# Layer 1's experts on the rows that chose them, for six of eight batches of a two-layer adaLN transformer

## What is computed

```python
h = layernorm(x) * (1 + ca) + sa
x = x + ga * attn1(h)              # 16 heads of 8 channels, relative bias, gate
h = layernorm(x) * (1 + cb) + sb
x = x + gb * ffn1(h)
# ffn1: a causal latent attention (MLA), then a mixture of 8 experts
def ffn1(x):
    x = x + mla(rmsnorm(x, g1))
    x = x + moe(rmsnorm(x, g2))
def moe(t):                        # t: tokens x 128
    top_v, top_i = top_k(t @ gate_w, 2)
    gates = softmax(top_v)
    combine = zeros(T, 8).at[rows, top_i].add(gates)
    hid = silu(einsum('td,edh->teh', t, w1))   # w1: 8 x 128 x 256
    ye = einsum('teh,ehd->ted', hid, w2)       # w2: 8 x 256 x 128
    return einsum('te,ted->td', combine, ye)
```

## Time and profile before

| what | us |
|---|---|
| median of 3 timed runs | 1957.47 |
| lowest and highest timed run | 1955.97 and 1969.35 |
| the profiled execution | 1974.12 |
| its span, first to last instruction | 1972.3 |
| first score matmul of slot 0, from the span's start | 692.2 |

### The profile page before, as it was taken

One profiled execution on the slowest core, in us unless ns is written; L12 is line 12 of the kernel. 1 busy time (PEld: TensorE's weight loads), 2 busy tenths in 40 slices (PEclk: granted clock), 3 DMA queues, 4 the chain that ended last, 5 costly groups with the idle time before them and its releaser, 6 DMA issues.

```text
span 1972.3 us, 46460 instructions
## 1 busy us (share of the span) xinstructions
PE 1737.1 (88%) x17489; PEld 1159.2 (59%) x17489; DVE 1428.1 (72%) x4507; ACT 1000.2 (51%) x2018; POOL 625.6 (32%) x871
## 2 busy tenths in 40 slices
PE   3898889898939479989999999999999999998997
PEld 2676767777726346545655655655555555655455
DVE  6777877787721267877887886887887787788756
ACT  2554455455513146647546636646645645644642
POOL 3111221111134147625514613613623522530000
PEclk6999999999969779979999999999999999999999
DMA  4522122211018222122212213123122122221111
...
DMA packets 109933, 144.31 MB, mean 73 GB/s; under 512 B 18752, under 2 KB 90880, under 8 KB 108432
## 3 DMA queue, kind: packets, MB, share of 16 engines
...
## 4 chain that ended last, share of the span: by engine, by line
PE 51%; DVE 11%; issue 3%; ACT 2%; DMA 1%; SPq 1%; ACTq 1%; POOL 1%; DVEq 0%; POOLq 0%
PE ps L1969 10%; PE ps L1954 8%; PE ps L2110 6%; PE ps L2008 5%; PE ps L2124 5%; PE ps L2019 4%; PE ps L1979 3%; DVE ps L2198 2%; PE ps L1225 2%; PE ps L1234 1%; DVE l_XY L2198 1%; PE ps L1981 1%; PE ps L2059 1%; DVE l_xn L2236 1%; PE ps L2039 1%
## 5 line engine op out<-in xcount | busy, mean ns | idle before, releaser
L1773 POOL TENSOR_SCALAR l_XY<-l_XY,l_nmax 128x512 f32<-128x512 f32 x512 | 388.8, 768 | 224.3 <-DVE l_nmax L2198 215.8
L2198 DVE CUSTOM_DVE_ANT_0 l_XY<-ps,strips 128x512 f32<-128x512 f32 x512 | 341.1, 687 | 140.6 <-PE ps L1954 136.8
L1954 PE MATMUL ps<-l_stack 72*128 72x512 bf16 (+3 forms) x1024 | 353.9, 351 | 65.7 <-DVE l_nmax L2198 53.8
L1830 ACT ACTIVATE PT<-ps 128x512 f32<-128x512 f32 x512 | 305.1, 599 | 197.4 <-PE ps L1969 184.7
L1969 PE MATMUL ps<-ident,l_XY 128*128 128x128 f32 x2048 | 319.0, 278 | 3.8 <-POOL l_XY L1773 3.0
L1969 PEld LDWEIGHTS ps<-ident,l_XY 128*128 128x128 f32 x2048 | 240.3, 141 | 110.5 <-ACT PT L1830 45.5
L2198 DVE CUSTOM_DVE_ANT_0 ps<-ps,mask 128x384 f32<-128x384 f32 (+3 forms) x512 | 245.2, 504 | 31.0 <-PE ps L1954 27.0
L1954 PEld LDWEIGHTS ps<-l_stack 72*128 72x128 bf16 x1024 | 102.0, 100 | 148.6 <-DVE l_nmax L2198 84.3
L1979 PE MATMUL ps<-l_stack 75*128 75x256 bf16 (+3 forms) x512 | 157.7, 310 | 13.1 <-ACT PT_odd L1838 6.0
L1838 ACT ACTIVATE PT_even<-ps 128x512 f32<-128x512 f32 (+1 forms) x256 | 120.9, 493 | 67.2 <-PE ps L1981 56.7
L2110 PE MATMUL ps<-l_fT,l_w_e 128*128 128x512 f32 x256 | 146.0, 659 | 2.6 <-DVE l_hid L2386 1.2
...
## 6 DMA issues: line engine op xcount, KB each, us to landing
...
l_w_e<-in_L_ffn_w_dram ACTq DMA_DIRECT2D x128, 128.0 KB
...
```

What stands on the lines that cost most here:

```text
L1773: nc.gpsimd.tensor_scalar(XY[:, c % XY_BUFS], XY[:, c % XY_BUFS], -1.0, nmax[:, c % 8:c % 8 + 1], ALU.mult, ALU.add).then_inc(y_pool, 1)
L1830: nc.scalar.activation(PT[:, quad(u, r), j], src.rearrange("p (k q) -> p k q", q=P), ACT.Exp).then_inc(moved, 1)
L1954: nc.tensor.matmul(ps[:, n % 3, 0:w], stack[0:STACK, 0, h, q * P:(q + 1) * P], stack[0:STACK, 1, h, 0:w], start=True, stop=True).then_inc( ...
L2198: nc.vector.tensor_tensor_reduce(out=dst, in0=src, in1=add, scale=-1.0, scalar=3.0e38, op0=ALU.add, op1=ALU.min, accum_out=low).then_inc(s ...
```

## The change

Batches 0 to 5 no longer run the experts densely. The rest of layer 1's mathematics is the same, and batches 6 and 7 keep the dense form.

1. **Router alone.** For a batch below 6 the place in the schedule holds only the projection, normalisation, logits and top-2 (`router`). A `fold` adds the scaled residual to `x` at once. New small VectorE operations and two or three bf16 matmuls count how many rows each expert has so far (`tally`, `place`), which gives each row two places in a DRAM tensor `rows_dram`. Eight indirect DMAs per batch on GpSimd scatter the 512 normalised rows there twice. Batch 2 and batch 5 have their router earlier, at place 38 of slots 7 and 13.
2. **Plan.** After the last router of a group (batches 0 to 2, then 3 to 5), five steps of VectorE work (`plan_blocks`) turn the counts into a list of 32 blocks: which 128 rows and which expert. 24 full blocks would hold 3072 rows; eight more cover the part-filled last block of each expert.
3. **Block pairs.** 16 pairs of blocks per group run in kind-1 slots, one pair every four steps: eight in slot 8, eight in slot 10, and 16 from place 18 of slot 14 to place 21 of slot 15. SP reads two numbers per block from the plan into registers and issues one DMA for 128 rows (64 KB) and one for the expert's weights (256 KB) from a table that it has copied together in DRAM. A pair is two transposes, eight fp32 matmuls of 128 columns (two records each), two ScalarE copies of 128x256, one tanh of 128x512, one VectorE product of 128x512, and a 128 KB store issued by ScalarE.
4. **Gather and add.** For each of the six batches, eight indirect DMAs on GpSimd bring the two results per row back, and VectorE weights and adds them: batches 0, 1, 2 in slot 12, batches 3 and 4 in slot 15, batch 5 after the last tile.
5. **Clearing and table.** SP clears `rows_dram` in six DMAs of 2 MB and builds the weight table (2 MB), in slots 0 to 5.
6. **Values.** `PT` has two buffers instead of three; the third one's memory holds part of the new tiles. `values` takes one buffer per call: the same number of column passes in matmuls of 128 columns instead of 256, twice as many instructions, one burst of 32 records every four steps instead of two bursts of 16 in every eight.
7. **SP's order.** SP's program follows the steps too, with the pair loads between `stack_up` and `store_parts`.

```diff
-MOE_START = {b: TILES * PLACE[1, b + 1] - 6 for b in range(B - 2)}
+GROUPS = ((0, 1, 2), (3, 4, 5))
+DENSE = (B - 2, B - 1)
+EARLY = [batches[-1] for batches in GROUPS] + list(DENSE)
+MOE_START = {b: TILES * PLACE[1, b] + TURN_AT[1] + 1 if b in EARLY else TILES * PLACE[1, b + 1] - 6 for b in range(B)}
...
+PAIR_STAGES = dict(load=-9, turn=0, evac=1, hidden=3, tanh=4, mul=5, out=6, copy=7)
+PAIR_WINDOWS = ((0, TILES * PLACE[1, 3] + 18, 8, 4), (0, TILES * PLACE[1, 4] + 18, 8, 4), (1, TILES * PLACE[1, B - 2] + 18, 16, 4))
...
+CLEAR_AT = (40, TILES + 20, 2 * TILES + 40, 3 * TILES + 50, 5 * TILES + 50)
+TABLE_AT = TILES + 40
+COMBINE = {0: TILES * PLACE[1, 5] + 2, 1: TILES * PLACE[1, 5] + 18, 2: TILES * PLACE[1, 5] + 34,
+           3: TILES * PLACE[1, B - 1] + 31, 4: TILES * PLACE[1, B - 1] + 47, 5: ALL + 2}
...
-V_AT, W_AT = 13, 32
+V_AT, W_AT = 10, 32
-XY_BUFS, QUADS, W_BUFS, VW = 5, 3, 3, HD + 2
+XY_BUFS, QUADS, E_BUFS, VW = 5, 2, 3, HD + 2
...
 # SP
+                def load_block_pair(n):
...
+                    wait_turned(sp, ("T", before))
...
+                    if n >= W_BUFS:
+                        sp.wait_ge(block_y_ready, n - W_BUFS + 1)
+                    for k in range(2):
+                        j = 2 * i + k
+                        at = nc.values_load(plan[0:1, g % 2, 0, j:j + 1], engines=(mybir.EngineType.SP,), ...
+                        e = nc.values_load(plan[0:1, g % 2, 1, j:j + 1], engines=(mybir.EngineType.SP,), ...
+                        sp.dma_start(x_b[:, n % X_BUFS, k, :], rows_dram[bass.ds(at, 1)]...
+                        sp.dma_start(w_b[n % W_BUFS][:, k, :], table_dram[bass.ds(e, 1)]...
...
 # GpSimd
+                def scatter(b, part):
...
+                    nc.gpsimd.indirect_dma_start(rows_dram.rearrange("n p c -> (n p) c"),
+                                                 bass.IndirectOffsetOnAxis(ap=row_index[:, k, t:t + 1], axis=0),
+                                                 xf[:, t, :], None, bounds_check=REGION_ROWS - 1,
...
 # TensorE
+                def block_hidden(n, m):
+                    pe.wait_ge(block_x_moved, n + 1)
...
+                    for i in range(2):
+                        for f in range(FT1):
+                            last = nc.tensor.matmul(ps[:, SIDE, (2 * i + f) * P:(2 * i + f + 1) * P],
+                                                    w_b[n % W_BUFS][:, i, f * P:(f + 1) * P], xT_b[:, n % 2, i, :], start=True, stop=True)
...
-                    for k in (2 * r, 2 * r + 1):
+                    for k in range(TT):
                         for j in range(4):
-                            last = nc.tensor.matmul(o[32 * j:32 * j + VW], v[:, k, 4 * head_group(s, g) + j, :], pair[:, :, j, k, :],
+                            last = nc.tensor.matmul(o[32 * j:32 * j + VW], v[:, k, 4 * head_group(s, g) + j, :], PT[:, quad(u), j, k, :],
...
 # ScalarE
-                for n in range(W_BUFS):
-                    expert(n)
...
+                def block_exponent(n):
+                    act.wait_ge(block_hid_ready, n + 1)
...
+                    nc.scalar.activation(hid_b[:, n % 2].rearrange("p i f s -> p (i f s)"), ps[:, SIDE, :], ACT.Tanh,
+                                         scale=0.5).then_inc(block_tanh, 1)
...
 # VectorE
+                def add_placed(b):
+                    n = COMBINED.index(b)
+                    dve.wait_ge(y_gathered, 16 * 2 * TT * (n + 1))
+                    link(nc.vector.tensor_tensor(y_tok[:, 0], y_tok[:, 0], bc(gates[:, b, 0].unsqueeze(2), wide), ALU.mult))
...
```

893 lines of the change are left out of this document (676 added, 217 removed).

## The result

The changed kernel takes 1980.63 us (median of 4, 1973.93 to 1985.8) against 1957.63 us beside it: ratio 1.0102, interval 1.0078 to 1.0126. It is slower by 1%. I had forecast 1932, faster by 1.3%. All ratios here are of fast runs alone; of the four runs of `spread` on its first chip two, the profiled one among them, were over 1.5% above its fastest and are left out of its ratio.

The account below looks back on a forecast made before the run. The prediction took the kernel to be bound by TensorE and priced it slot by slot; its terms summed to -25 us, giving 1932 for the median of 1957.47, likeliest 1915 to 1952, range 1893 to 1985.

Parts of the forecast that it names:

- Slots 4 and 6: Layer 1 slots left with only routers: slot 2's 53.6 us plus 4, so 57.6 against 73.6, -16.0 each, sum -32.
- Slot 12: Router 4 us and three adds 7 us on top of slot 2, gathers free: 64.6 against 72.5, -8.
- Slots 8 and 10: Eight pairs each at 1.15 us a step add 10 us, plan or router 2.5: 66 against 72.7, sum -13.
- Slot 14: Slot 2's 53.6 plus 11 for batch 7's preparation, pairs over 46 steps and 1: 80 against 83.8, -4.
- Slot 15 with the tail: Last pairs in 22 steps +7, adds of batches 3 and 4 +3, batch 5's add in the tail 0.
- Slots 7 and 13: Early routers of batches 2 and 5 in slots full of PE work: +4 each, sum +8, bounds +2 and +8.
- Values: 128-column matmuls, twice the instructions, cost little over eight slots: +2 taken, bounds -1 and +5.
- Rival D: In the values, twice the records take twice the time: +125 us, 2057; chance 0.02.
- SP's queue: SP issuing pair loads and register reads, 4.9 us a pair, falls behind in slot 14: +10, bounds 0 and over 100.
- Rival A: SP becomes the bound: a register read of 1.2 us makes a pair 7.6 us on SP; 1997 us, chance 0.15.
- Rival B: Everything overlaps well: pair steps at 1.07 us, adds hidden in DVE's idle time, SP keeps up; 1902 us, chance 0.22.
- Rival C: Light slots 4, 6 and 12 fall to 1.2 GHz and are not shorter than before: 1970 us, chance 0.08.

Follow-up runs that it names:

- spread: Changed kernel with gathers and adds of batches 0 to 2 moved, so no gather meets a scatter and adds wait longer: 1970.75 us, 1.0074; on another chip 1.018.
- nogather: Changed kernel without the gathers of all six batches and VectorE's wait for them, the adds running on zeros: 1990.2 us, slot 12 at 66.7.
- noadd: Changed kernel without the gathers and the adds of all six batches, expert results unused: 1963.1 us, slot 12 at 63.1.
- router8: Changed kernel with batch 2's router back in slot 8 and five pairs moved from slot 8 to slot 10: 1987.36 us against 1984.03.
- warm: Changed kernel with each score matmul of slots 2, 4, 6 and 12 issued twice: 1983.57 us against 1984.03.

## Why the prediction was wrong

The method carried: the slots one by one, slot 2 as a direct measurement of a slot without experts. Where it was applied to a slot like slot 2 it held. Three of the prices put on top failed: a wait taken as nothing, a step taken as the mean of its slot, and a router taken at half its cost.

- *Slots 4 and 6*: 57.6 each forecast, 55.6 and 56.5 in the profile, 55.6 to 63.1 over the three. Right, and with more scatter than I allowed for.
- *Slot 12*: this is the step that failed most, by 19 us. I put the gathers "beside an engine that is busy only 6.17 us there", at no cost. The engine was free, but an add in VectorE's queue waits for eight of its DMAs, and 8 x 1.31 us don't fit in 12 steps, nor 16 of them in 12. That wait costs 10 us at the same clock, 17 with the clock that nogather was granted. I had the 1042 ns of one gather in the earlier trace rows and multiplied it by nothing; the 0.30 us to the next is in that row too, as its 10.1 us of "issue" over 32. The adds' work, which I priced at 7 us, measures 4 to 10. What is left of the slot, 63.1 us with a router alone, stands against my 57.6, as slot 6 does where it is at the lower clock for longer.
- *Slots 8 and 10*: the pairs' 10 us each was right to 0.6 us. The base was wrong: 58.9 and 60.0 without pairs, where I had 56.1. Whether that is the router's or plan's work or the clock (37.5 and 30.7 us at 1.2 GHz there) was not taken apart.
- *Slot 14*: the slot without pairs is 64.3, as forecast (53.6 + 11). The pairs cost 19 to 25, not 14, and only PE's 1.8 us for a pair's weights is traced.
- *Slot 15 with the tail*: +23.2 against +10. The pairs cost 14.4 and not 7, since the step beneath is 0.65 and not the mean 0.84; the gathers and adds cost 9.6 (noadd against after, with 11.2 and 20.5 us at 1.2 GHz) and not 3. My step was the mean over a slot whose parts have different limits, the mistake that I warn of in my own first paragraph for the whole kernel.
- *Slots 7 and 13*: +13.7 against +8. Each early router costs 8 us by router8 where I had 4, less 1 us by which all kind-0 slots are shorter; the sum of 13.7 lies above my upper bound of 8. I counted its 2 us of PE; it is 4.2, and VectorE's 8.9 us give the rest as waits.
- *Values*: -3.6 over the four undisturbed kind-0 slots in place of +1, below my lower bound of -1 for all eight. Rival D (2057) is refuted.
- *Clearing and table*: +0.5. Right.
- *SP's queue*: +10 forecast, some 2 measured. In the kernel after a pair is on SP like this:

```profile
1760.12 0.33 SPq L1878 DMA_DIRECT2D l_XY<-rows_dram  x1
1760.64 0.33 SPq L1879 DMA_DIRECT2D w_b<-table_dram  x1
1761.75 0.33 SPq L1878 DMA_DIRECT2D l_XY<-rows_dram  x1
1762.27 0.33 SPq L1879 DMA_DIRECT2D w_b<-table_dram  x1
```

An issue of this shape takes 0.33 us, not the 0.69 of `stack_up`; the register loads have a median of 270 ns (L1874 and L1876, 64 each); a pair is some 3.3 us on SP against four steps of 4.7. Rival A (1997) is refuted. A small part of it came true: at step 60 of slot 14 PE waits for a pair's weights, 1.8 to 2.6 us in every profile that has pairs there. In the kernel after SP issues that pair's loads behind six of `stack_up`. SP's timeline, and PE's wait in the steps that follow:

```profile
1787.44 4.24 SPq L1836 DMA_DIRECT2D l_stack<-parts_dram  x6
1793.02 0.36 SPq L1878 DMA_DIRECT2D l_XY<-rows_dram  x1
```

```profile
PE ps L2408 <- DMA w_b<-table_dram: 1.8, 1, 1.8
```

The Trainium skill, "Runtime: NRT & Kernel Launch", section "Instruction fetch mechanics", has about 200 ns per register; the trace is a third above that. The ~1.3 us of its preamble breakdown, which the same section calls several registers' worth, is not the price of a read here.

- *Rival B* (everything overlaps, 1902) is refuted by the waits above, and most of all by slot 12's.
- *Rival C* (the light slots fall to 1.2 GHz, 1970) had 0.08 and was in part the case: 24 to 41 us of time at 1.2 GHz in slot 4 or 6 where there were 7, worth 0 to 7 us in each of the light slots as it falls. It did not take back what these slots had gained, as the rival had it. The Trainium skill, "TensorE: Matmul & The Clock Gate", section "What's actually happening", calls the throttled state the default that activity releases; warm agrees, with more matmuls and less time at 1.2 GHz (10.2 us against 23.9 to 30.7 in slot 4).

The terms of layer 1 missed by +19 (slot 12), +13 (15 with the tail), +10 (14), +6 (8 and 10), +6 (7 and 13), and -4, -6, -2 and -10 for slots 4 and 6, values, clearing and SP: together +32, from -25 to +7.7. The other 15 us up to the medians' +23 are in no term: they are what separates one profiled execution from the median, in opposite directions for the two kernels. My range ended at 1985 and held the result, but for no reason that I had given: its upper end was there for rival A and rival C, and the loss came from a wait, the pairs and the routers. That is luck; the centre was off by 49, and the time moved the other way, to which I had given a chance of 0.20.

Taking 218 us of work from the busiest engine gave back some 91 us by the estimate above (its 95 less the values' 3.6), since PE no longer bounds the slots that held it; by the terms of my sum the same slots had 98, so that part held. What I put in its place and around it cost 103, where my terms had 73: 41 for the pairs, 10 for SP, 10 for the adds, 8 for the routers, and 2 each for the clearing and the values. No version with all its work that I ran beats the kernel before. The nearest is spread, at 1.0074.
